# Gated cross-attention with experts on one core: the weights' sum of squares on ScalarE in four pieces per expert, at other places of the attention step

## The reference, cut to what matters

```python
# x (16, 112, 256), ctx_768 (16, 375, 192), 16 heads of 16
x = x + tanh(g_xattn) * attention(layernorm(x), ctx_768, mask) @ Wo
# 8 experts, top 2; gate_w and up_w (8, 256, 512), down_w (8, 512, 256)
probs = softmax(xn @ router_w.T), the best 2 kept and normalised
h = silu(xn @ gate_w[e] + gate_b[e]) * (xn @ up_w[e] + up_b[e])
x = x + tanh(g_ffn) * sum_e probs[e] * (h @ down_w[e] + down_b[e])
```

## Time and profile before

| what | value |
|---|---|
| median of 3 runs | 614.59 us |
| the profiled execution | 619.51 us |
| its span, first to last instruction | 617.8 us |
| mean granted TensorE clock | 0.908 |
| busy: PE, DVE, ACT, POOL | 496.9, 429.3, 334.8, 289.9 us |
| attention stage with its set-up, in the trace | about 0 to 364 us |
| steps 4 to 15, in the trace | about 112 to 326 us |

### The profile page before, as it was taken

How to read it: one execution, slowest core, us unless ns; L and a number is a source line. 1 busy time by engine, 2 the same in 40 slices (tenths; PEclk the granted TensorE clock), 3 DMA queues, 4 the chain that set the end, 5 groups by cost and what they waited for, 6 DMA issues and landing times. The chain is left out here.

```text
span 617.8 us, 15147 instructions
## 1 busy us (share of the span) xinstructions
PE 496.9 (80%) x4738; PEld 448.0 (73%) x4739; DVE 429.3 (69%) x906; ACT 334.8 (54%) x623; POOL 289.9 (47%) x251
## 2 busy tenths in 40 slices
PE   2477798999999999999989933198879999999930
PEld 2366687888888888888877832087869999999930
DVE  1745578999899898999998558577785555545520
ACT  2232265766667666666765565176676555455420
POOL 9400365445555654545566320333465655666340
PEclk9997689999999999999996565589999999999985
DMA  8336745566455645546330349865543434433234
GB/s 186 94 82 169 164 111 117 163 171 164 114 153 135 158 105 160 162 102 167 90 87 1 99 141 307 260 189 134 141 88 60 70 61 68 64 55 60 28 42 127
DMA packets 68974, 74.88 MB, mean 121 GB/s; under 512 B 28696, under 2 KB 57200, under 8 KB 68736
## 3 DMA queue, kind: packets, MB, share of 16 engines
q1 hardware_dynamic: 60864, 63.22, 38.7%
q0 software_dynamic: 8064, 11.06, 11.1%
HBM read 42.51 MB, written 14.98 MB: 93 GB/s over the span
## 5 line engine op out<-in xcount | busy, mean ns | idle before, releaser
L343 POOL TENSOR_TENSOR PL<-PT 125x448 f16<-125x448 f32 x96 | 99.8, 1041 | 134.5 <-ACT PT L459 134.4
L723 DVE TENSOR_REDUCE mx<-bank 112x1 f32<-112x375 f32 x256 | 130.9, 543 | 28.2 <-PE bank L557 26.9
L459 ACT ACTIVATE PT<-bank 125x448 f32<-125x448 f32 x192 | 103.8, 544 | 84.8 <-PE bank L572 84.0
L1312 POOL DMA_INDIRECT acc_scr<-ys,slot_row x42 | 68.7, 1637 | 83.3 <-ACT ys L1352 74.4
L557 PE MATMUL bank<-KS,QS 97*112 97x376 f32 x256 | 91.8, 381 | 13.0 <-DVE mx L723 10.5
L572 PE MATMUL bank<-QS,KS 98*125 98x256 f32 x384 | 87.1, 313 | 3.1 <-DMA QS<-nm 2.3
L572 PEld LDWEIGHTS bank<-QS,KS 98*125 98x125 f32 x384 | 69.5, 202 | 4.3 <-DMA QS<-nm 2.5
L1386 PE MATMUL bank<-xH,GH 128*128 128x256 f16 x336 | 64.8, 275 | 8.1 <-ACT sg L1337 7.8
L557 PEld LDWEIGHTS bank<-KS,QS 97*112 97x112 f32 x256 | 46.2, 185 | 25.6 <-DVE mx L723 21.8
L1386 PE MATMUL bank<-xL,GH 128*128 128x256 f16 x336 | 64.6, 274 | 0.0
L1386 PE MATMUL bank<-xH,GL 128*128 128x256 f16 x336 | 64.4, 273 | 0.0
(11 more groups left out here) (213 smaller groups left out, 1088.5 us busy)
## 6 DMA issues: line engine op xcount, KB each, us to landing
KS<-kH SPq DMA_DIRECT2D x128, 94.0 KB, 2.2
KS<-kL SPq DMA_DIRECT2D x64, 94.0 KB, 2.1
QS<-q_scr SPq DMA_DIRECT2D x96, 56.0 KB
ctx_sb<-in_ctx SPq DMA_DIRECT2D x16, 281.2 KB
wsq<-in_L_ffn_gate_w SPq DMA_DIRECT2D x8, 512.0 KB, 3.7
wsq<-in_L_ffn_up_w SPq DMA_DIRECT2D x8, 512.0 KB, 4.4
w_raw<-in_L_ffn_gate_w SPq DMA_DIRECT2D x8, 512.0 KB, 4.8
w_raw<-in_L_ffn_up_w SPq DMA_DIRECT2D x8, 512.0 KB, 4.2
```

Of the source, the lines that this page charges most:

```text
L343: pool.tensor_tensor(PL[:, 2 * k:2 * k + 2, :, 0:N], PT[:, 2 * k:2 * k + 2, :, 0:N], PH[:, 2 * k:2 * k + 2, :, 0:N], ALU.subtract).then_in ...
L459: act.activation(PT[:, 2 * k:2 * k + 2, :, 0:N].rearrange("p a e i -> p (a e) i"), psST[k % 2][0:JP].rearrange("p (a i) -> p a i", i=NI)[: ...
L723: dve.tensor_reduce(mx[:, hd:hd + 1], psS[hd % 2][0:N, 0:M], AX.X, ALU.max).then_inc(v_max, 1)
L1312: pool.indirect_dma_start(acc_scr, bass.IndirectOffsetOnAxis(ap=slot[:, TH * t + k:TH * t + k + 1].bitcast(U32), axis=0), ys[:, u, k, :], ...
```

## The change

The buffer sq gets four columns per expert. ACT squares an expert's wsq in four operations of 128 x 512 elements (gate rows 0 to 127, gate rows 128 to 255, then the same of up) instead of one of 128 x 2048. They stand behind the exponential of slots 8 and 11, and in slots 13 and 14, which have no exponential; in slot 14 the piece stands behind the variance. Each piece has its own sum. SP's load of the next expert waits for all four pieces of the one before. At the start of the expert stage PE sums the four columns with four accumulating matmuls.

```diff
--- before.py
+++ after.py
@@ -70,7 +70,7 @@
 
         mv2 = keep("mv2", [N, B, 2], F32)
         routed = keep("routed", [N, B, router_w.shape[0]], F32)
-        sq = keep("sq", [128, router_w.shape[0]], F32)
+        sq = keep("sq", [128, router_w.shape[0], 4], F32)
         banks = [whole.enter_context(nc.psum_tensor(f"bank{i}", [128, 512], F32)) for i in range(6)]
         misc = whole.enter_context(nc.psum_tensor("misc", [128, 1024], F32))
         psS, psST, psO = banks[0:2], banks[2:4], banks[4:6]
@@ -192,7 +192,7 @@
         ST, AG, XC, XT, LG, RT = 5, 14, 7, 11, 12, 13
 
         V1, VR, V2, LV = 3, 3, 6, 6
-        SQ = 4
+        SQ = (8, 11, 13, 14)
         MT, OT, OP, CT = 8, 9, 12, 10
 
 
@@ -275,7 +275,7 @@
                     e = squared(i, c)
                     if e is not None:
                         sp.wait_ge(s_clear, CLEARED + 2)
-                        wait(sp, a_sq, e)
+                        wait(sp, a_sq, len(SQ) * e)
                         for j, w in enumerate((gate_w, up_w)):
                             sp.dma_start(wsq[:, j], w[bass.ds(e, 1)].rearrange("o (c p) f -> p (o c) f", p=128)
                                          ).then_inc(i_sq, 16)
@@ -436,12 +436,6 @@
                             act.wait_ge(g_r, b + 1)
                             act.activation(VS[:, u, :, :, HD:2 * HD].rearrange("p t h d -> p (t h) d"),
                                            vr[:].rearrange("p t (h d) -> p (t h) d", d=HD), ACT.Copy).then_inc(a_V2, 1)
-                        if k == SQ and squared(i, c) is not None:
-                            e = squared(i, c)
-                            act.wait_ge(i_sq, 32 * (e + 1))
-                            act.activation(wsq[:].rearrange("p j c f -> p (j c f)"),
-                                           wsq[:].rearrange("p j c f -> p (j c f)"), ACT.Square,
-                                           accum_out=sq[:, bass.ds(e, 1)]).then_inc(a_sq, 1)
                         if k == OT + 1 and live(i, c, 3):
                             b, h, u = at(i, c - 3)
                             act.wait_ge(p_OT, b + 1)
@@ -459,6 +453,12 @@
                             act.activation(PT[:, 2 * k:2 * k + 2, :, 0:N].rearrange("p a e i -> p (a e) i"),
                                            psST[k % 2][0:JP].rearrange("p (a i) -> p a i", i=NI)[:, :, 0:N],
                                            ACT.Exp).then_inc(a_E, 1)
+                        if k in SQ and squared(i, c) is not None:
+                            e, part = squared(i, c), SQ.index(k)
+                            act.wait_ge(i_sq, 32 * (e + 1))
+                            act.activation(wsq[:, part // 2, part % 2], wsq[:, part // 2, part % 2], ACT.Square,
+                                           accum_out=sq[:, bass.ds(e, 1), part:part + 1].rearrange("p o a -> p (o a)")
+                                           ).then_inc(a_sq, 1)
                         if k == V1 and live(i, c, 1):
                             b, h, u = at(i, c - 1)
                             act.wait_ge(a_V, b + 1)
@@ -1081,7 +1081,9 @@
                 def _(pe):
                     pe.wait_ge(q_k, 1)
 
-                    pe.matmul(bN[:, 0:E], ones[:], sq[:], start=True, stop=True).then_inc(t_n, 1)
+                    for part in range(4):
+                        mm = pe.matmul(bN[:, 0:E], ones[:], sq[:, :, part], start=(part == 0), stop=(part == 3))
+                    mm.then_inc(t_n, 1)
                     pe.wait_ge(i_sm, 32)
                     for j in range(2):
                         mm = pe.transpose(bC[:, 32 * j:32 * j + E * FC], braw[:, j, :], ident[0:E * FC, 0:E * FC])
```

## The result

| | median | lowest to highest | executions |
|---|---|---|---|
| before | 614.34 us | 612.78 to 615.0 | 4 |
| after | 624.01 us | 620.53 to 626.3 | 4 |

The change makes the kernel slower: ratio 1.0134 [1.0079, 1.0189]. The forecast was 617.8 us with a range up to 619.5, so the sign was right and the size was not.

A forecast was written before the change was run, and what follows sets the result against it. The prediction took PE's waits for other engines' results to bound the attention steps. Loop +0.2 us and steps 4 and 14 +3.0 us gave +3.2 us: 614.59 + 3.2 = 617.8 us, range 614.4 to 619.5.

The forecast's parts named there:

- The loop, 6 x (0.51 - 0.48): Six squared loop steps: 0.51 us lost by later xcT, 0.48 gained as xc no longer meets POOL; +0.2 us.
- Steps 4 and 14, xc behind POOL: Straight steps: POOL starts before DVE's row-mean subtraction xc, so PE waits 1.47 us before head 15.
- taking the square away should turn a wait of 0.48 us into one of 1.47 us: 2 x 0.99 = +2.0 us: Steps 4 and 14: PE's wait before head 15 grows by 0.99 us each, taken from plain straight step 15.
- differ in length only by PE's waits: Attention stage: steps run on PE, and only PE's waits make their lengths differ.
- "Cost nothing" for SP: SP's next expert load comes 3.8 us later, queue gaps take up 3.6, nm 0.2 late against 2.4 slack.
- SP becomes the bound: SP's queue gaps absorb nothing, nm 1.4 us late in four steps, 5.6 us on top: 623.4 us; chance 0.03.
- Slot 11: Piece between last exponential and xcT delays PE's router product 0.61 us, 0.10 absorbed: 0.51 us in each of 8 steps.
- 8 x 0.51: Slot 11's piece delaying xcT and the router product over all eight squared steps: 4.1 us.
- Pieces: ACT: each 512-element piece takes 0.63 us, four hold ACT for 2.45 us in place of 1.9.
- Expert stage: Three more matmuls over sq, at most 1.8 us, beside PE's 7.28 us DMA wait: cost 0.
- slots 8, 13 and 14: ACT pieces there are covered while PE works through scores and waits: cost nothing.
- From the profile to the median: Profiled 619.51 us would become 622.7; the +3.2 us difference was carried over to the unprofiled median 614.59.

The follow-up runs named there:

- e5: The changed kernel with slot 11's piece moved to slot 14 (pieces in slots 8, 13, 14, 14): 620.2 us, ratio 1.0032 to before.
- e1: The changed kernel run again unaltered: 620.77 us, ratio 1.013 to before.
- e4: The changed kernel with the four pieces of steps 4 and 14 together in slot 4: 619.05 us, ratio 1.004 to before.
- e7: The changed kernel with SP's load of wsq issued behind the queries, ahead of the key moves: 622.76 us, ratio 1.009 to before.
- e10: e9 with xc, DVE's row-mean subtraction, back in slot 7: 616.65 us, ratio 0.9998 to before.
- e12: e9 with SP's load of wsq back at the head of the step: 611.64 us, ratio 0.9904 to before.
- e9: e8 run again on another chip, as base for putting single things back: 608.95 us, ratio 0.9852 to before.
- e6: The changed kernel with pieces in slots 8, 13, 14, 14 and xc in slot 10: 613.69 us, ratio 0.989 to before.
- e8: The changed kernel with pieces in slots 8, 13, 14, 14, xc in slot 10, SP's load behind the queries: 606.53 us, ratio 0.9822 to before.
- e11: e9 with a piece back in slot 11 (pieces in slots 8, 11, 13, 14): 612.83 us, ratio 0.9945 to before.
- e2: The changed kernel with xc, DVE's row-mean subtraction, in slot 10 instead of 7: 614.48 us, ratio 0.9963 to before.

## Why the prediction was right or wrong

- **The loop, 6 x (0.51 - 0.48).** Right as a difference, apart from step 5 (see SP). xc takes 0.34 to 0.35 us in all nine loop steps, PE's wait before head 15 is gone there, and PE waits up to 0.8 us for xcT. Steps 6 to 13 together change by -0.33 us against a forecast of +0.2. Each term alone shows in steps 8 and 11 of e5, which has neither the collision nor the piece in slot 11: 0.60 and 0.46 us below before, 0.59 and 0.45 below after. One reading was loose: xc does not end as POOL ends, it ends 0.16 us later (195.03 against 194.87), and in step 15 it ends 0.15 us behind POOL's operation.
- **Steps 4 and 14, xc behind POOL.** Right in place and as a wait: 1.49 us against 1.47 forecast, decided by 20 and 10 ns. The rule that the forecast drew on from the Trainium skill (SBUF — State Buffer, Who interferes with whom), that the first to issue holds the shared port, agrees with these rows down to 10 ns.
- **The step that failed: "taking the square away should turn a wait of 0.48 us into one of 1.47 us: 2 x 0.99 = +2.0 us."** The sum ended at the wait, on the premise that the steps "differ in length only by PE's waits", which gives the clock a price of nothing. Behind it the clock goes to 0.50, and the two steps grew by 2.63 and 3.35 us in place of 1.5 each: 3.0 us missed. The nearest row, step 15 of before, gave no warning: behind its wait of 1.47 us the clock stayed at 1.00 for 9 us more, and it does so in after too (17.85 us both). In e1, e4, e5, e7 and e10 the clock falls behind the wait of step 15 (19.1 to 20.4 us). Where there is no collision step 15 takes 16.43. So this one step shows both prices: 1.4 us for the wait, and 1.2 to 2.6 us more where the clock falls. In steps 4 and 14 it fell in all five profiles with the 1.49 us wait, and the forecast's range had no place for that.
- **"Cost nothing" for SP** failed in step 5: +1.0 us in the profile. The gaps of 3.6 us were counted with the issues at the length that they had. In after two of them were 1.24 and 1.44 us longer, so nm came 3.2 us later and not 0.2. The rival "SP becomes the bound" was given 0.03 and named four steps. It came true in one of them there, and in one or two of some other executions. The medians price it at 2.7 us (e12 against e9) and 7.2 (e6 against e8), both with intervals that overlap; why these differ was not settled.
- **Slot 11.** The wait is as forecast. As a price in whole executions it is 3.9 us (e11 against e9), near the 4.1 of 8 x 0.51, but its steps show only 1.0, so the agreement proves little.
- **Pieces.** 0.62 us each and four in 2.45 us, as worked out from the rows. The figure of 93 ns of fixed time that the Trainium skill (Perfetto Trace Analysis, Optimizing Scalar/DVE Operations) gives would have made it 2.2 us (an estimate). The traces have 0.20 us for the separate operation that reads the sum out.
- **Expert stage** and slots 8, 13 and 14: nothing, as forecast. From the first `scores_T` of step 17 to the end it is 273.0 us in both profiles.
- **From the profile to the median.** The forecast carried a difference of one execution over. The profiled steps give +6.65 us, the ratio 1.0134 gives 8.2 (4.9 to 11.6). The four executions of after took 620.53, 622.61, 625.42 and 626.3 us at mean clocks of 0.919, 0.909, 0.906 and 0.898. In the 29 executions of before on chip A those above 0.920 took 611.3 to 616.8 us, those at 0.901 or less 621.3 to 627.3. So time tends to go with the clock in these two sets, though not in every one: in e11 the execution at 0.902 took 611.42 us, that at 0.919 took 613.42. That the changed kernel has more falls is shown for steps 4 and 14 (after and e1), and for step 7 in e1. What decides over those in steps 15 to 17 and in the expert stage stays open, and so does what is left of the 8.2 us beyond the steps.

## What to carry to other kernels

A wait of PE is not priced by its length alone. The wait of 1.47 us in step 15 cost 1.4 us where the clock stayed and 2.7 to 4.0 where it fell behind it. Waits of 0.47 and 0.60 us brought the clock down in two executions, and one of 0.84 left it up in another. So the sum must go on past the wait, with the fall of the clock as a cost that may or may not come. When an operation is moved, look at what each engine starts beside what, above all where two starts lie within 0.1 us, and move the partner too: xc alone gave 1.004, the square alone 1.013, both together 0.996, and with the piece out of slot 11 and the load moved behind the urgent issues 0.982 and, on another chip, 0.985. A queue's gaps can be worth less than their length: here two of its issues took 1.2 and 1.4 us longer once the load came later, for a reason that was not found.

## What the runs showed of the hardware that was not expected

- The granted clock fell to 0.50 soon behind single PE waits of 0.47 us (e12), 0.60 (e6), 0.78 (e4), 1.02 (e12) and 1.49 (after), and behind two of 0.74 and 0.57 with 1.2 us of work between them (e1), in the middle of steps in which PE is otherwise over 90% busy. It stayed at 1.00 behind the waits of 0.46 to 0.56 of before, behind those of 0.66 to 0.76 for xcT (after, e11), behind 0.75 and 0.84 in a row (after) and 0.75 and 0.63 (e2). Behind the 1.47 to 1.49 us of the collision it stayed in two cases of 17, both in step 15. So the length of one wait does not decide alone; what does was not found.
- Step 16, in which nothing is squared, took 14.84 to 14.99 us at full clock and 16.96 to 19.02 where the clock fell in it (all 14 profiles). No edit of this case aimed at that fall.
- The same DMA issue on SP took 0.41 us or 1.65 us, four kL moves 2.51 or 3.96. The mean DMA share over the moves was not higher in the long case (0.51) than in the short one (0.63).
- One source of differences between executions of one kernel: nm is late in another step each time, and where the clock falls behind it the next step is about 1.5 us longer (e1, e6, e12).
